# A GNN kernel: the first pass of a message layer takes two tiles per turn of TensorE's loop

## The reference

```
h = x @ W_enc.T + b_enc
for l in range(2):
    m = concatenate([h[row], h[col]], axis=-1)
    m = relu(m @ msg_W1[l].T + msg_b1[l])
    m = m @ msg_W2[l].T + msg_b2[l]
    agg = segment_sum(m, col, num_segments=h.shape[0])
    upd = concatenate([h, agg], axis=-1) @ upd_W[l].T + upd_b[l]
    h = layer_norm(h + upd, ln_g[l], ln_b[l])
return h @ W_out.T + b_out
```

## Time and profile before

| what | value |
|---|---|
| median of 2 runs | 4371.71 us (4367.15 to 4376.27) |
| the profiled execution's own time | 4388.74 us |
| its span, first to last instruction | 4387.0 us |
| mean granted TensorE clock | 0.913 |
| PE, PEld, DVE, ACT, POOL busy | 84%, 74%, 72%, 44%, 16% |

### The profile page before, as it was taken

One profiled execution on the slowest core, in us unless ns is written; L12 is line 12 of the kernel. 1 busy time (PEld: TensorE's weight loads), 2 busy tenths in 40 slices (PEclk: granted clock), 3 DMA queues, 4 the chain that ended last, 5 costly groups with the idle time before them and its releaser, 6 DMA issues.

```text
span 4387.0 us, 283020 instructions
## 1 busy us (share of the span) xinstructions
PE 3695.7 (84%) x110515; PEld 3226.4 (74%) x110515; DVE 3147.9 (72%) x10135; ACT 1949.2 (44%) x3725; POOL 722.4 (16%) x1709
## 2 busy tenths in 40 slices
PE   2777777679989999558998999956999998998997
PEld 1555555368878889428887889845888888997997
DVE  6999997756656666866665666688888875556555
ACT  0222222434434444334443444424666665555554
POOL 0111112100001111110000111112333231112221
PEclk9778777589999999759999999977999999999999
DMA  3000000167777787027776777703444438895984
GB/s 58 5 6 5 5 6 16 43 186 212 219 200 205 212 216 210 0 71 199 214 214 195 212 216 214 198 10 106 148 148 148 148 112 241 273 275 147 275 274 120
DMA packets 483680, 654.03 MB, mean 149 GB/s; under 512 B 147732, under 2 KB 324093, under 8 KB 483610
## 3 DMA queue, kind: packets, MB, share of 16 engines
q1 hardware_dynamic: 448741, 622.54, 48.8%
q0 software_dynamic: 9600, 19.68, 2.5%
q10 hardware_dynamic: 25269, 10.99, 1.0%
HBM read 537.51 MB, written 115.47 MB: 149 GB/s over the span
## 4 chain that ended last, share of the span: by engine, by line
PE 63%; DVE 15%; issue 10%; DMA 9%; DVEq 1%; ACT 1%; SPq 1%; ACTq 0%; POOLq 0%; POOL 0%
PE psum L968 19%; PE psum L1170 14%; PE psum L1157 9%; PE psum L972 6%; PE psum L986 6%; DMA arena<-rows_stacked 3%; PE psum L1137 3%; DMA rows_stacked<-tabf 3%; PE psum L1374 3%; DMA arena<-table_a,ovcur 2%; DVE arena L746 1%; DVE AGGf L739 1%; DVE Hf L1483 1%; PE psum L1145 1%; DVE AGGf L744 1%
## 5 line engine op out<-in xcount | busy, mean ns | idle before, releaser
L968 PE MATMUL psum<-tabf,arena 125*32 125x128 bf16 x60384 | 1396.1, 220 | 166.6 <-DMA arena<-rows_stacked 107.1
L968 PEld LDWEIGHTS psum<-tabf,arena 125*32 125x32 bf16 x60384 | 1210.8, 97 | 294.4 <-issue 195.5
L972 PE MATMUL psum<-arena 96*32 96x128 bf16 x20928 | 1257.8, 222 | 5.3 <-issue 5.3
L1006 ACT ACTIVATE arena<-psum 128x512 f32<-128x512 f32 x1300 | 779.9, 600 | 998.4 <-PE psum L972 998.4
L1022 DVE TENSOR_SCALAR arena<-tabf,row 125x512 bf16<-125x512 bf16 x1312 | 466.0, 355 | 593.6 <-PE psum L972 538.4
L972 PEld LDWEIGHTS psum<-arena 96*32 96x32 bf16 x20928 | 704.1, 96 | 7.3 <-issue 1.4
L1170 PE MATMUL psum<-tabr,cellr 125*125 125x256 f32 x5000 | 616.1, 283 | 34.2 <-DVE tabr L1613 34.2
L1170 PEld LDWEIGHTS psum<-tabr,cellr 125*125 125x125 f32 x5000 | 599.7, 187 | 34.6 <-issue 34.6
L986 PE MATMUL psum<-arena 128*32 128x129 f32 x10400 | 557.8, 278 | 3.4 <-issue 3.4
L1157 PE MATMUL psum<-tabf,arena 125*125 125x384 bf16 x2500 | 511.9, 327 | 0.0
L1088 ACT CAST cellr<-arena 125x630 fp32r<-125x630 bf16 x500 | 360.0, 720 | 255.2 <-PE psum L1170 236.9
(11 more groups left out here) (203 smaller groups left out, 4796.3 us busy)
## 6 DMA issues: line engine op xcount, KB each, us to landing
arena<-cells_kept SPq DMA_DIRECT2D x500, 315.0 KB, 3.8
tabf<-slots_turned SPq DMA_DIRECT2D x408, 384.0 KB, 5.1
tabf<-slots_turned SPq DMA_DIRECT2D x306, 288.0 KB, 5.0
cells_kept<-arena SPq DMA_DIRECT2D x625, 126.0 KB, 1.7
tabf<-slots_turned SPq DMA_DIRECT2D x102, 512.0 KB, 4.8
arena<-rows_stacked SPq DMA_DIRECT2D x404, 96.0 KB, 3.4
table_a<-tabf SPq DMA_DIRECT2D x50, 187.5 KB
rows_of_h<-Hf ACTq DMA_DIRECT2D x15, 560.0 KB
```

The source lines that it names most:

```text
L968: pe.matmul(psCell[b][q:q + GW, g * D:(g + 1) * D], fr, rows, start=g == 0 and p == 0, stop=False, tile_position=(0, q), skip_group_check= ...
L972: m = pe.matmul(psCell[b][q:q + GW, g * D:(g + 1) * D], toB[:, b, g * CELL + q:g * CELL + q + GW], cur[:, part_of(at), g, :], start=g == 0 ...
L1006: act.activation(msgs[:, SLOT[pos], :, 0:D], psCell[SLOT[pos]].rearrange("p (c d) -> p c d", d=D), ACT.Relu).then_inc(f_msg, 1)
```

## The change

In the first pass (`h == 0`) of both message layers, TensorE's loop turns 25 times in place of 50, and its body holds the visits of two tiles, with tile numbers i * 2 and i * 2 + 1. The gathers ahead of the loop stay, and so does the second pass. No other engine's code is touched.

```diff
                 pe.wait_ge(f_msg, visit_base(kk))
                 for pos in range(2):
                     gather(0, pos)
+                if h == 0:
+                    with pe.Fori(0, NT // 2) as i:
+                        for w in range(2):
+                            for pos in range(n):
+                                gather(i * 2 + w, pos + 2)
+                                scatter(i * 2 + w, pos)
+                    continue
                 with pe.Fori(0, NT) as i:
                     for pos in range(n):
                         gather(i, pos + 2)
```

## The result

The changed kernel takes 5362.98 us (5359.57 to 5366.4, 2 runs) against 4371.71: ratio 1.2263, 95% interval 1.2228 to 1.2298, 991 us slower. The profiled execution has a span of 5357.8 us, 970.8 more than before. Matmuls and weight loads are the same in number as before, 110515 each, and all instructions are 125 fewer; the code queue is what differs.

A forecast was written before the change was run, and what follows sets the result against it. TensorE's instruction stream was taken to bound the first passes; 4388.7 + 186 - 24 - 10.5 + 13.4 = 4553.6 us profiled, so 4537 us, 3.8% slower; forecast range 4408 to 4687, 8-in-10 range 4360 to 5260.

The forecast's parts named there:

- each block has one fixed place, only these two change places: First-pass loops: the ninth block displaces only the first, one 3.87 us wait per jump back, +186 us; chance 0.34.
- Rival 2: First-pass loops: the oldest block is thrown out, so all eight come late each turn, +869 us, 5240 us; chance 0.33.
- Absorbed waits: First passes: stacked rows' transfers and one-hots catch up while TensorE stands, taking off 24 us for the two passes.
- Loop ends: TensorE's first-pass loops: fifty fewer ends at 0.21 us each save 10.5 us, bounds 9.5 and 11.5.
- what is removed: Prediction's section on TensorE's first-pass loops: 25 turns instead of 50 per pass, saving 10.5 us of loop ends.
- Cold blocks: First turns of the first passes: seven more stalls on new code blocks at 1.91 us each, +13.4 us.
- nothing is lost: First-pass loops: all needed blocks stay, leaving only -10.5 and +13.4 us, 4375 us, with scatter 4360 to 4392; chance 0.27.
- Second passes: Second passes of both layers: their times stay the same in every case, as their loop isn't touched.

The follow-up runs named there:

- e2: The changed kernel with its two-tile loops starting 20 instruction slots into a code block; 4601.98 and 4521.36 us.
- e6: The changed kernel with jump-back hints, plus second passes at two tiles a turn from a block's start, also hinted; 4507.04 us, 1.0124 of the kernel before.
- e1: The changed kernel with its two-tile loops starting exactly at a code block's start; 4415.21 us, 1.0074 of the kernel before.
- e8: The changed kernel with loops at a block's start, no hint, and first-pass stacked rows loaded one tile further ahead into four buffers; 4416.37 us, ratio 0.9926.
- e3: The changed kernel, loops in the same place, with a hint on the jump back; 4407.39 us, 1.0052 of the kernel before.
- e7: As e6, but without the hint in the second passes; 5546.76 us, 1.2465 of the kernel before.
- e9: The kernel before, without any edit, profiled again on the chip of e8; 4455.91 us.
- e5: As e8, but with the hint on the jump back of the first-pass loops; 4424.74 us, 0.9946 of the kernel before.

## Why the prediction was wrong

- **The step that failed** is the forecast's "each block has one fixed place, only these two change places". It gave one wait of 3.87 us a turn, 186 us in all, and a time of 4537 us; the runs showed all eight blocks fetched anew in each turn, 20.3 us a turn more than before. The count behind it was right: seven crossings, eight blocks, a ninth asked for ahead; the changed trace has seven stalls beside the one at the jump, and nine packets a turn. What the ninth throws out was open, and I gave 0.34 to one lost block per turn and 0.33 to all of them, so which of the two was the forecast was close to a toss. The runs show all: nine packets a turn in the changed kernel, nine or none in e2. Rows read before spoke to neither, as no loop there lost a block; nor did they show that a ninth block has to take another one's place, with six kept by the count. In e6 eight stayed, and in the changed kernel eight and one ahead did not. Rival 2's "the oldest goes" fits the packet counts: in a loop the oldest of eight blocks is the one needed next. As said, the counts don't exclude the other two ways.
- **Rival 2's price** was 5240 us, measured 5363. I took 4.2 us from asking for a block to running it, from first turns; in a turn of 35.8 us it is 35.8 / 8 = 4.5 us. In the turn shown above the seven crossings lie 4.0 us apart, as I took them, but over the jump back it is 7.1 us (958.52 to 965.65): the mis-sized part is the jump. 48 x (35.8 - 15.5) = 974 us, the span's difference within 4. My range ended at 5260, as it took in rival 2 only to its middle.
- **Absorbed waits:** the wait for stacked rows does vanish under the stalls, worth little against them; in layer 0 10.7 us of waits for VectorE's one-hots stand in its place. The fall of the granted clock to 0.80 was not in my sum. What it costs of its own, no run shows.
- **Loop ends:** 0.21 us each was right in size (e1: 0.48 us at the loop's end, 0.22 elsewhere), but it doesn't arrive: against the 5 us saved in a pass, e1's wait for the stacked rows' transfer is 10.7 us longer in layer 0. In "what is removed" I treated TensorE's saving as the kernel's. With the rows loaded ahead (e8) the first passes fall to 370.2 and 384.5 us, from 400.5 and 401.6 on the same chip.
- **Cold blocks:** +13.4 us forecast. In e1 the "issue" waits in first turns are 10.9 and 17.8 us where the kernel before has 7.3 and 6.2, +15. With the rows' longer wait this makes its first passes 407.3 and 415.6 us, 8.1 and 16.8 more, and the rival "nothing is lost" would have been 4404 by e1's ratio (4371.71 x 1.0074), not 4375, and above its own 4392.
- **Second passes** were to keep their times; they do within 2.1%.

## What to carry to other kernels

Count the instructions of an unrolled TensorE loop (in these traces loads and matmuls are one each, and the 4 f32 matmuls of L986 are 8, with 8 loads) and the blocks that a turn touches where it lies. I took 256 instructions a block, estimated from the 123 and 124 matmuls between stalls and as many loads; the packets of e1, e6 and e7 agree with it. With the one fetched ahead they had to be at most eight in these runs, or the whole turn was fetched again, here 20 us a turn (in e2 in 8 of 48 turns). The queue of instruction packets tells it at once, by its count and by nine packets per turn. The loop that fills seven blocks was saved by placing its head at a block's start (e1: 38 packets); the ones that need all eight were saved by the hint on the jump back (e3: 37, e6: 46), where placing alone left nine packets a turn (e7: from 1399 to 1437 us, 478 in all). But look first at which transfer a faster turn will wait for.

## What the runs showed of the hardware

- Eight blocks are kept, and by my count all of eight can be used: e6's second-pass turn of some 2037 instructions ran with no packet on q8 from 1360 to 1800 us with the hint (46 in the whole execution), and was fetched anew each turn without (e7: 478, nine of them from 1399 to 1437 us).
- One block too many cost all the others: seven and one ahead took 38 packets in all (e1), eight and one ahead 469 (the changed kernel). Of the two turns of e2 shown, one takes 16.0 us with no packet, the other 38.4 us with nine.
- The same kernel differed between chips in one kind of stall. On e9's chip each turn of the second pass stops for 0.5 us on "issue", at the same place of the turn to within a matmul (those at 1405.57 and 1415.04 us, one turn apart). These are its waits from 1345 to 1755 us; the kernel before had 3.2 us on another chip, and e5, on a third one, has 22.1 us in the same 0.5 us stops:

```profile
PE psum L968 <- issue: 11.7, 23, 0.5
PE psum L972 <- issue: 10.9, 21, 0.5
```

Fetched code is not the cause: e9 has the same 30 packets in all as the kernel before. What holds TensorE at that place stays open.
